# Register loads of the sparse loops: without bound checks, on clamped tables, and in small pieces

## The reference

```
h = relu(layernorm(x))                                  # 6250 x 512
el, er, v = projections of h; e = leaky_relu(el[src] + er[dst])     # 8 heads per edge
a = exp(e - max over dst) / sum over dst
x = x + segment_sum(v[src] * a, dst)                    # graph attention
h = relu(layernorm(x))
twice: h = relu(segment_sum((h @ W)[src] * norm, dst) + (h @ W) * 2/deg + b)   # graph convolution
x + h
```

## Time and profile before

| | |
|---|---|
| median of 3 runs | 5284.48 us (5274.53 to 5292.15) |
| the profiled execution | 5270.99 us, span 5269.2 us |
| TensorE, VectorE, ScalarE, GpSimd busy | 3765, 2207, 2146, 2638 us (71, 42, 41, 50% of the span) |
| mean granted clock of TensorE | 0.86 |
| DMA over the span | 797.8 MB, 151 GB/s |

### The profile page before, as it was taken

How to read it: one execution, slowest core, us unless ns; L and a number is a source line. 1 busy time by engine, 2 the same in 40 slices (tenths; PEclk the granted TensorE clock), 3 DMA queues, 4 the chain that set the end, 5 groups by cost and what they waited for, 6 DMA issues and landing times.

```text
span 5269.2 us, 76662 instructions
## 1 busy us (share of the span) xinstructions
PE 3764.7 (71%) x15765; PEld 2124.8 (40%) x15766; DVE 2206.7 (42%) x3996; ACT 2146.0 (41%) x5272; POOL 2638.0 (50%) x2776
## 2 busy tenths in 40 slices
PE   4510399967676777778967777777897777787774
PEld 3300399445555555654422322333343223332331
DVE  6200288845556566667522222222253222222224
ACT  3200155234444444444434444444443444444445
POOL 2567300045555555553366666666503666666663
PEclk8755699988888888989989888988998898888997
DMA  6510022455555555555566566666514666565667
GB/s 241 145 22 4 18 59 74 153 179 165 156 161 153 151 153 158 161 150 173 192 175 174 169 171 174 176 170 175 162 69 148 176 175 173 171 173 168 172 174 241
DMA packets 330313, 797.80 MB, mean 151 GB/s; under 512 B 88175, under 2 KB 110337, under 8 KB 329327
## 3 DMA queue, kind: packets, MB, share of 16 engines
q0 software_dynamic: 201184, 630.92, 42.3%
q1 hardware_dynamic: 111839, 134.27, 7.9%
q10 hardware_dynamic: 17232, 31.99, 1.9%
HBM read 711.56 MB, written 84.98 MB: 151 GB/s over the span
## 4 chain that ended last, share of the span: by engine, by line
PE 49%; issue 20%; another core or an unknown queue 13%; DVE 6%; SPq 4%; ACT 4%; DVEq 2%; DMA 1%; ACTq 1%; POOL 0%; POOLq 0%
PE mm L1675 12%; PE tr L1675 11%; PE mm L1504 6%; SPq L1083 3%; PE mm L1596 3%; PE tr L1596 3%; PE mm L1652 3%; PE sm L1652 3%; PE sm L1541 2%; PE tr L1652 2%; ACT eler_hots L1419 2%; PE hist_ps L1652 2%; DVE edge L836 2%; PE tr L1499 1%
## 5 line engine op out<-in xcount | busy, mean ns | idle before, releaser
L1278 POOL DMA_INDIRECT edge<-h_tab,row_idx x1564 | 1477.9, 945 | 1128.7 <-SPq L1089 436.2
L1675 PE MATMUL mm<-edge,eler_hots 128*128 x1760 | 936.7, 678 | 344.1 <-issue 106.2
L1419 ACT ACTIVATE eler_hots<-eler_hots,ones 128x256 f32<-128x256 f32 x1320 | 663.8, 503 | 1224.8 <-remote 398.0
L1675 PE MATMUL tr<-edge,eler_hots 128*128 x1760 | 907.7, 661 | 259.8 <-SPq L1077 81.5
L1278 POOL DMA_INDIRECT rows_wmat<-v_tab,row_idx x782 | 738.9, 945 | 575.1 <-SPq L1089 348.4
L1410 ACT ACTIVATE eler_hots<-iota,ndrel 128x128 f32<-128x128 f32 x2640 | 916.4, 394 | 168.6 <-issue 5.2
L1675 PEld LDWEIGHTS mm<-edge,eler_hots 128*128 128x128 f32 x1760 | 363.7, 215 | 903.9 <-issue 903.5
L862 DVE TENSOR_TENSOR big<-big,mm 128x512 f32 x440 | 302.5, 688 | 928.9 <-PE mm L1675 463.6
L1675 PEld LDWEIGHTS tr<-edge,eler_hots 128*128 128x128 f32 x1760 | 361.3, 211 | 780.8 <-issue 780.5
L862 DVE TENSOR_TENSOR big<-big,tr 128x512 f32 x440 | 302.6, 688 | 881.5 <-PE tr L1675 385.6
L1652 PE MATMUL mm<-edge,eler_hots 128*128 128x260 f32 x1176 | 413.4, 437 | 242.4 <-ACT eler_hots L1419 133.5
(11 more groups left out here) (229 smaller groups left out, 3516.1 us busy)
## 6 DMA issues: line engine op xcount, KB each, us to landing
h_tab<-rows_wmat SPq DMA_DIRECT2D x98, 256.0 KB, 2.0
edge<-h_tab,row_idx POOLq DMA_INDIRECT x1564
rows_wmat<-low_tab SPq DMA_DIRECT2D x133, 128.0 KB
ht_tab<-rows_wmat SPq DMA_DIRECT2D x49, 256.0 KB
big<-ht_tab ACTq DMA_DIRECT2D x49, 256.0 KB
v_tab<-rows_wmat ACTq DMA_DIRECT2D x49, 256.0 KB
x_tab<-big SPq DMA_DIRECT2D x49, 256.0 KB, 2.1
rows_wmat<-v_tab,row_idx POOLq DMA_INDIRECT x782
```

The source lines that it names most:

```text
L1278: pool.indirect_dma_start(ring[:, 2 * u + i, :], None, tab, bass.IndirectOffsetOnAxis(ap=row_idx[:, b, n:n + 1], axis=0)).then_inc(a["rows ...
L1419: act.activation(onehot[:, s.j % 2, :, :], dist[:, :, :], ACT.Relu, bias=ones[:, 0:1], scale=-1.0).then_inc(a["onehot_set"], 1)
L1675: last = pe.matmul(sum_ps[bank][:, :], onehot[:, s.j % 2, n, :], edge[:, ds(slot[0][s.j] + n * D, D)], start=(n == 0), stop=(n == 1))
```

## The change

The two tables that were checked when read (`need_i`, and `first_i`, from which `ends_tab` comes) are clamped to their bounds when they are made, and all loads in the loops are now without assertions. Where such a value is waited for, it is masked with `WORD`. In `aggregate_weighted` on VectorE and in `aggregate` on TensorE the loads are cut into pieces of 2 to 4 values, placed behind the work of single steps; `aggregate` on TensorE has turns of 16 steps in place of 8. In SP's `relay` the load stands ahead of the wait for landed rows. SP waits for the tables before the first relay.

```diff
--- before.py
+++ after.py
@@ -57,6 +57,7 @@
 GPAD = -(-J // IDX) * IDX
 LAG = 2
 OFFS = 8
+WORD = 1023
 MSGS = 3
 PAIRS = 3
 WB = 12
@@ -528,7 +529,7 @@
                 did(dve.scalar_tensor_tensor(counted, row[:, 0, 0:GROUPS], 1.0, row[:, 1, 0:GROUPS], ALU.add, ALU.subtract))
                 did(dve.tensor_tensor_scan(summed, ones[0:1, 0:1].to_broadcast([1, GROUPS]), counted, 0.0, ALU.mult, ALU.add))
                 did(dve.tensor_tensor(row[:, 0, 0:GROUPS], summed, counted, ALU.subtract))
-                did(dve.tensor_copy(first_i, summed))
+                did(dve.tensor_scalar(first_i, summed, 1.0, float(SP), ALU.max, ALU.min))
                 marks["ends_of_units"] = prep[0]
                 did(dve.tensor_tensor(summed, row[:, 1, 0:GROUPS], row[:, 0, 0:GROUPS], ALU.subtract))
                 did(dve.tensor_copy(row[:, 1, 0:1], summed[:, 0:1]))
@@ -627,7 +628,7 @@
             did(dve.tensor_copy(cols[:, 0:2, :], tr[1][:, 0:2 * blocks].rearrange("p (b v) -> p v b", v=2)))
             did(dve.tensor_scalar(gidx[:, :], cols[:, 0, :], -1.0, None, ALU.add))
             marks["gidx"] = prep[0]
-            did(dve.tensor_copy(need_i[:, :], cols[:, 0, :]))
+            did(dve.tensor_scalar(need_i[:, :], cols[:, 0, :], 1.0, float(UNITS), ALU.max, ALU.min))
             did(dve.tensor_scalar(slotcol_i[0][:, :], gidx[:, :], float(SIXTH), None, ALU.mult))
             did(dve.tensor_scalar(slotcol_i[0][:, :], slotcol_i[0][:, :], 16, None, ALU.arith_shift_right))
             did(dve.tensor_copy(cols[:, 4, :], slotcol_i[0][:, :]))
@@ -807,41 +808,59 @@
             dve.wait_ge(v_sum, TILES)
             did(dve.memset(big[:, scanned:ringed], 0.0))
 
-            def load_offs(k):
+            def load_offs(k, n=OFFS):
 
                 return nc.values_load_multi_w_load_instructions(
-                    slot_i[0:1, ds(k, OFFS)], engines=(mybir.EngineType.DVE,), min_val=0,
+                    slot_i[0:1, ds(k, n)], engines=(mybir.EngineType.DVE,), min_val=0,
                     max_val=(TILES - 1) * AW, skip_runtime_bounds_check_because="clamped when the table is made")[1]
 
             def aggregate_weighted(a):
-                offs, need, slot = [None], [None], [None]
+                offs, need, slot = {}, {}, {}
+
+                def load_needs(s, pair, n):
+                    n = n if s.inner else min(n, SP // 2 - (s.turn * WB + pair))
+                    if n > 0:
+                        _, got = nc.values_load_multi_w_load_instructions(
+                            need_row[:, ds(s.turn * WB + pair, n)], engines=(mybir.EngineType.DVE,), min_val=1, max_val=UNITS,
+                            skip_runtime_bounds_check_because="clamped when the table is made")
+                        need.update({pair + m: value for m, value in enumerate(got)})
+
+                def load_slots(s, at, n):
+                    k = s.k + (at - s.j)
+                    n = n if s.inner else min(n, SP - k)
+                    if n > 0:
+                        _, got = nc.values_load_multi_w_load_instructions(
+                            slot_row[0][:, ds(k, n)], engines=(mybir.EngineType.DVE,), min_val=0,
+                            max_val=(RING[0] - 1) * 2 * AW, skip_runtime_bounds_check_because="masked when the table is made")
+                        slot.update({at + m: value for m, value in enumerate(got)})
 
                 def step(s):
-                    if s.j % OFFS == 0:
-                        if s.live():
-                            _, need[0] = nc.values_load_multi_w_load_instructions(
-                                need_row[:, ds(s.turn * WB + s.j // 2, OFFS // 2)],
-                                engines=(mybir.EngineType.DVE,), min_val=1, max_val=UNITS)
-                            _, slot[0] = nc.values_load_multi_w_load_instructions(
-                                slot_row[0][:, ds(s.k, OFFS)], engines=(mybir.EngineType.DVE,), min_val=0,
-                                max_val=(RING[0] - 1) * 2 * AW, skip_runtime_bounds_check_because="masked when the table is made")
-                        offs[0] = load_offs(s.k)
+                    if s.j == 0:
+                        load_needs(s, 0, 2)
+                        load_slots(s, 0, 2)
                     if s.live():
                         weights = w_ps[s.j // WB][:, s.j % WB, :].rearrange("p (c h) -> p c h", c=2)
                         if s.j % WB == 0:
                             dve.wait_ge(w_ps_set, s.turn * 2 + (s.j // WB + 1))
                         if s.j % 2 == 0:
-                            dve.wait_ge(a["rows_ready"], need[0][s.j % OFFS // 2])
-                        got = rows_wmat[:, ds(slot[0][s.j % OFFS], 2 * AW)].rearrange("p (c n) -> p c n", c=2)
+                            dve.wait_ge(a["rows_ready"], need[s.j // 2] & WORD)
+                        got = rows_wmat[:, ds(slot[s.j], 2 * AW)].rearrange("p (c n) -> p c n", c=2)
                         dve.tensor_tensor(msgs[:, s.j % MSGS, :, 0:D].rearrange("p c (h f) -> p c h f", f=F),
                                           got[:, :, 0:D].rearrange("p c (h f) -> p c h f", f=F),
                                           weights.unsqueeze(3).to_broadcast([P, 2, H, F]), ALU.mult).then_inc(msg_set, 1)
+                    if s.j % 4 == 1:
+                        load_slots(s, s.j + 1, min(4, 2 * WB - 1 - s.j))
+                    elif s.j % 4 == 2 and s.j + 2 < 2 * WB:
+                        load_needs(s, s.j // 2 + 1, 2)
+                    elif s.j % 4 == 3 or s.j == 0:
+                        n = 3 if s.j == 0 else min(4, 2 * WB - s.j)
+                        offs.update({s.j + m: value for m, value in enumerate(load_offs(s.k, n))})
                     if s.live(LAG):
                         w, bank = s.k - LAG, (s.j - LAG) % PAIRS
                         dve.wait_ge(a["step_sum"], w + 1)
                         if s.past(1, LAG):
                             dve.wait_ge(a["acc_added"], 2 * w)
-                        o = offs[0][s.j % OFFS]
+                        o = offs[s.j]
                         for half, bank_ps in enumerate((sum_ps[bank], half_ps[bank])):
                             part = big[:, ds(o + half * (AW // 2), AW // 2)]
                             dve.tensor_tensor(part, part, bank_ps[:, 0:AW // 2], ALU.add).then_inc(a["acc_added"], 1)
@@ -1073,19 +1092,19 @@
 
                 def step(s):
                     g, u = s.k, s.j % units
-                    sp.wait_ge(a["rows_in"][u], s.turn * (2 * PER_IDX // units * 32) + (s.j // units * 32 + 32 + a["rows_before"][u]))
-                    sp.sem_inc(a["rows_ready"], 1)
-                    if s.j % PER_IDX == 0 and (s.inner or g + PER_IDX < UNITS):
-                        load_idx((s.turn * 2 + (s.j // PER_IDX + 1)) * IDX, (s.j // PER_IDX + 1) % 2)
                     if s.j % 4 == 0:
                         lo = freed if not s.inner and g == 0 else 0
                         n = 4 if s.inner else min(4, UNITS - g)
                         _, ends = nc.values_load_multi_w_load_instructions(
                             ends_row[:, ds(g + lo - freed, n - lo)], engines=(mybir.EngineType.SP,), min_val=1,
-                            max_val=SP)
+                            max_val=SP, skip_runtime_bounds_check_because="clamped when the table is made")
                         free[0] = (None,) * lo + tuple(ends)
+                    sp.wait_ge(a["rows_in"][u], s.turn * (2 * PER_IDX // units * 32) + (s.j // units * 32 + 32 + a["rows_before"][u]))
+                    sp.sem_inc(a["rows_ready"], 1)
+                    if s.j % PER_IDX == 0 and (s.inner or g + PER_IDX < UNITS):
+                        load_idx((s.turn * 2 + (s.j // PER_IDX + 1)) * IDX, (s.j // PER_IDX + 1) % 2)
                     if s.past(freed):
-                        sp.wait_ge(done, free[0][s.j % 4])
+                        sp.wait_ge(done, free[0][s.j % 4] & WORD)
                         sp.sem_inc(a["slot_free"], 1)
                         if refill and not s.inner and g - freed >= UNITS - units:
                             for c in range(2):
@@ -1122,6 +1141,7 @@
                 sp.dma_start(by_part[:, at], edge[:, at]).then_inc(w_kept, 16)
 
 
+            sp.wait_ge(tabs_in, 64)
             relay(agg[0], msg_set)
             load_idx(0, 0)
             sp.wait_ge(msg_set, SP)
@@ -1655,27 +1675,45 @@
                 pipelined(pe, SP, 4 * PAIRS, 0, step)
 
             def aggregate(a):
-                need, slot = [None], [None]
+                need, slot = {}, {}
+
+                def load_needs(s, pair, n):
+                    at = s.turn * OFFS + pair
+                    n = n if s.inner else min(n, SP // 2 - at)
+                    if n > 0:
+                        _, got = nc.values_load_multi_w_load_instructions(
+                            need_row[:, ds(at, n)], engines=(mybir.EngineType.PE,), min_val=1, max_val=UNITS,
```

(29 more changed lines are left out.)

## The result

The changed kernel takes 5291.2 us (median of 12 runs, 5272.3 to 5304.0), the kernel before, run beside it, 5275.2 us: a ratio of 1.0034, 95% interval 1.002 to 1.0048. It is 0.3% slower. 5100 us had been forecast in a range to 5300, with 0.12 for slower.

The account below looks back on a forecast made before the run. Consumers (VectorE, TensorE, ScalarE, SP's relay) were taken to set the pace. Terms of 410 us, capped and less 52 us returned, left 324; times 0.56 gave 181 off 5271, plus 13 for the runs' median: 5100 us, range 4900 to 5300.

Parts of the forecast that it names:

- What bounds the kernel now: Three aggregations: GpSimd needs 972 and 976 us by itself; its 348 and 219 us slot waits mean consumers set the pace.
- What is given back: Aggregations: denser DMA traffic lengthens VectorE's remote waits, so part of the removed pauses is lost, leaving 181 us.
- the linear gain: All three aggregations: 324 us left of the removed pauses after 52 us more remote waits; 0.44 of it taken as lost.
- the traffic eats it: Rival: loads and relay become quick, but remote waits grow by 240 to 376 us; 5150 to 5284 us, chance 0.20.
- the linear law: Aggregations: remote share of a stage grows 0.19 points per GB/s of traffic, 52 us more remote waits.
- VectorE's term: First aggregation: spreading VectorE's unchecked loads behind queued multiplies removes its issue waits, gain 136 us.
- The cap: First aggregation: TensorE is next at 951 busy plus 214 remote, 1165 us, so the stage gives at most 155 us.
- The size of a short load: VectorE's register loads in the first aggregation: 0.10 us plus 0.063 an element, 0.22 us for two, 0.35 for four.
- TensorE's term: Convolutions: loads in pieces and turns of 16 remove the issue waits ahead of the mm banks, 49 and 43 us.
- SP's term: SP's relay: an unchecked load ahead of rows_ready gains 53 us in the first aggregation, 79 and 50 in the convolutions.
- The clock: TensorE in the convolutions: 755 us at full speed against 900 busy, so up to 145 us each hang on idle stretches.

Follow-up runs that it names:

- e1_dve: Kernel before with only VectorE's part of the change, its first-aggregation loads unchecked and in pieces; 0.998 of the kernel before.
- e12_after_again: The changed kernel, unaltered, run again in a batch where the kernel before takes some 4095 us; 4088.6 us, 0.9991 of the kernel before.
- e17_before_half_gather: Kernel before with the second gather of each unit left out in all three aggregations, everything else at full work; 3690.2 us.
- e18_after_half_gather: Changed kernel with the second gather of each unit left out in all three aggregations, everything else at full work; 3504.6 us.
- e4_before_narrow: Kernel before with every gather moving 128 of a row's 512 numbers, as many gathers for a quarter of the bytes; 0.9989 of the kernel before.
- e11_before_again: The kernel before, unchanged, run again for a profile in a batch where it takes some 4095 us; 4092.3 us.
- e3_pe: Kernel before with only TensorE's part of the change, loads in unchecked pieces and turns of 16; 1.0011 of the kernel before.

## Why the prediction was wrong

**What bounds the kernel now: here the first step failed.** The text worked out that GpSimd alone needs 972 and 976 us a stage, took its 348 and 219 us of waits for slots as proof that the consumers set the pace, and then took the consumers' named pauses for what stretches the stage. Removing these pauses left GpSimd's waits where they were (394 and 211 us). The text had named the sign for this, a first stage unchanged with the issue row gone, as meaning that TensorE and not VectorE sets its pace. `e1_dve` shows that sign (22 us of issue, 1319 us), and the first stage does get shorter with less work on TensorE. Where GpSimd is never held, it takes 992 to 995 us per stage in either kernel. For the 4095 us kind the cause is shown, by `e12_after_again`, `e17_before_half_gather` and `e18_after_half_gather`: the loads are hidden under the gathers.

**What is given back: the size was wrong, and so was the cause.** 0.44 of the linear gain was to be lost; in fact all of it was. The 0.44 also counts twice: it came from the growth of the remote share from 16.2 to 19.4%, from which the 52 us of the linear law had been taken already. The remote rows together rose from 675 to 1058 us, above the 900 that had been named as the sign. That is the outcome of the rival "the traffic eats it" (0.20), but not its mechanism, which `e4_before_narrow` and `e11_before_again` refute. Its upper end, 5284, was also 7 us under the time. That 5291 lies within the range up to 5300 is luck, for no step of the text leads there. And the remote rows were no quantity to scale: in the convolutions they grew by nearly what the named waits for the same count lost.

**VectorE's term.** Forecast 136 us, capped at 155 with SP's. The cap added TensorE's 951 us of work to a wait of VectorE (214), and so is no sum of one engine. In the profile after, 103 us of issue waits are gone and the stage did not get shorter; with the gathers halved the term is worth 97 us. The mechanism was right, the size in the uncovered kernel 0.7 of the forecast, the value here nothing.

**The size of a short load was wrong.** 0.22 us had been worked out for two elements and 0.35 for four. The profile after has, for the needs (two each) and the slots (two or four) on VectorE:

```profile
L823 DVEq TENSOR_LOAD <-src_flat x110: 518/535/778, 1089.2 to 2434.0; - x110
```

```profile
L832 DVEq TENSOR_LOAD <-src_flat x129: 520/964/983, 1090.0 to 2439.2; - x129
```

The line through the earlier trace rows did not hold once the loads were cut up. The floor of about 600 ns in the Trainium skill, "DMA: Bandwidth & Descriptors", section "Latency and other measured facts", is nearer for these, though not for the 347 ns of the earlier trace rows. It did no harm: the multiply covered them, as the 6.7 us of `e18_after_half_gather` show.

**TensorE's term.** 49 and 43 us, taken whole; with the gathers halved the stages lose 48 and 45. That the sizes agree is partly chance: with the gathers halved the issue row in front of the `mm` banks is 5.8 us, and most of the pauses that the loads make stand under other names. Here the term is worth nothing (`e3_pe`: 1.0011).

**SP's term.** 53, 79 and 50 us of gain were forecast. Nothing of it came: alone it costs 0.85%. With the gathers halved it was not run by itself, but VectorE's and TensorE's blocks of loads account for most of the 190 us, and VectorE's wait for SP's relay did not fall (24.5 and 29.6 us). The shares that L1083 had on the chain of waits were no gain to be had. The bound of 0 that the text had named was the right end, and that it could be below 0 was not considered.

**The clock.** Its mean went from 0.860 to 0.855 and gave nothing. The 900 us of TensorE's busy time against 755 at full speed were read as time to be won. At a clock of 0.99 TensorE is still busy 809 us, and the stage is GpSimd's.

**What stays open.** For the 5275 us kind three things are shown: the bursts of slow register instructions on every queue but GpSimd's, the late counts beside them, and that GpSimd's waits for slots keep a convolution near 1200 us whether TensorE has less work, the loads of TensorE and SP are cut, or fewer bytes move. My reading is that GpSimd is the bound between the bursts too, and is held only through them, when the rings are full; a load removed elsewhere then moves nothing. Against it stands that in the first stage less work on TensorE shortens the slot waits, and that twice as many slow instructions did not lengthen a convolution. A rival is left: the ring in which ScalarE's two one-hot buffers wait for TensorE's late count and TensorE waits for ScalarE would hold the consumers whatever is taken from VectorE. Neither was tried: the halved gathers ran only in batches of the other kind, and no run has more one-hot buffers. Neither what sets off the bursts nor why a quicker SP lengthens the first stage (by 74 us alone, by 38 with the others, by nothing where there are no bursts) is settled; the bytes moved and the place of the load are ruled out, and GpSimd's lead may have a part.

## What to carry to other kernels

When an engine sits at a nearly fixed own time plus waits, ask what ends those waits and whether the change shortens that. A pause of another engine is worth something only if it lies in the chain that frees the slot, and taking half of the bound engine's work out tells in one run what is hidden under it. Add up all the waits for one semaphore, with and without a visible cause, by stage, before you scale one of them: if one row grows by what its neighbour loses, only the name has changed.

## What the runs showed of the hardware

- Register loads cut into pieces are not cheaper by the element: 535 ns for two and 964 for four, against 347 for four and 599 for eight as blocks.
- The same kernel takes 4092 or 5275 us. In the slower kind register and semaphore instructions of SP, ScalarE and TensorE, and a few of VectorE, take some 0.7 us in bursts, and GpSimd's never do (998 records in the profile before, none of them on GpSimd). Of the 1185 us between the profiles of the kernel before (`e11_before_again` for the quicker kind) 427 lie ahead of the first aggregation and 741 in the three (all 782 gathers of each counted); what lies between the first two aggregations takes the same, 206 us against 208.
- A quarter of the gathered bytes changed no stage by over 1% (1317, 1210 and 1205 us against 1319, 1201 and 1201): a gather costs GpSimd 0.945 us and 0.30 between two, at 40 GB/s as at 215.
